# Accumulating DMAs from GpSimd in place of loads and sums, in a two-layer kernel with experts

## The reference

```python
xn = _layernorm(x)
s = _L0_attn_ref(xn, ...)
g = _silu(moe_experts(xn) + shared_mlp(xn))     # 8 of 64 experts per token, weighed, and the shared one
x = x + s * g
xn = _layernorm(x)
s = _L1_attn_ref(xn, ...)                       # causal attention over the batch axis of 2
g = _silu(_L1_ffn_ref(xn, ...))                 # two ternary linear layers with a gelu between
x = x + s * g
```

## Time and profile before

| | us |
|---|---|
| median of 3 timed runs | 412.49 (409.43 to 412.79) |
| the profiled execution | 405.89 |
| its span, first to last instruction | 404.1 |
| busy in the span: PE / DVE / ACT / POOL | 330.5 / 316.3 / 215.1 / 235.5 |

### The profile page before, as it was taken

One profiled execution on the slowest core, in us unless ns is written; L12 is line 12 of the kernel. 1 busy time (PEld: TensorE's weight loads), 2 busy tenths in 40 slices (PEclk: granted clock), 3 DMA queues, 4 the chain that ended last, 5 costly groups with the idle time before them and its releaser, 6 DMA issues.

```text
span 404.1 us, 6961 instructions
## 1 busy us (share of the span) xinstructions
PE 330.5 (82%) x2044; PEld 252.1 (62%) x2044; DVE 316.3 (78%) x989; ACT 215.1 (53%) x540; POOL 235.5 (58%) x219
## 2 busy tenths in 40 slices
PE   0999777989978989998898889970189888898893
PEld 0994344656666777776676667750068776787772
DVE  4589887766978888577878887742878998889975
ACT  3763535353544535854545454520286768766681
POOL 3610066666757877787887888762275765653311
PEclk9999999999999999999999999986589999999998
DMA  7965955667748899888877886557800000000001
GB/s 256 394 210 162 372 156 144 134 132 158 169 114 196 200 290 231 204 213 195 196 175 169 166 182 146 90 63 174 270 0 2 28 27 2 26 28 28 18 11 53
DMA packets 34041, 58.41 MB, mean 145 GB/s; under 512 B 3835, under 2 KB 20563, under 8 KB 33875
## 3 DMA queue, kind: packets, MB, share of 16 engines
q1 hardware_dynamic: 21715, 39.08, 30.1%
q0 software_dynamic: 12288, 18.88, 26.1%
HBM read 40.22 MB, written 17.73 MB: 143 GB/s over the span
## 4 chain that ended last, share of the span: by engine, by line
PE 32%; DVE 24%; issue 14%; POOL 11%; DMA 11%; ACT 7%; POOLq 0%; DVEq 0%; ACTq 0%
DMA acc_d<-W,idxE 8%; POOL acc_d L496 5%; PE two L1712 5%; POOL W L477 3%; PE two L1398 3%; PE two L1446 3%; PE two L1523 2%; PE two L1679 2%; PE two L1456 2%; PE two L1555 2%; PE two L1588 2%; DVE W L1106 2%; PE two L1474 2%; DVE WoS L977 2%; PE two L1408 2%
## 5 line engine op out<-in xcount | busy, mean ns | idle before, releaser
L496 POOL DMA_INDIRECT acc_d<-W,idxE x64 | 102.0, 1593 | 37.1 <-DVE W L1106 22.3
L477 POOL DMA_INDIRECT W<-tok_d,idxE x56 | 57.0, 1018 | 46.5 <-DVE idxE L1061 29.7
L707 ACT ACTIVATE W<-two 128x256 f32<-128x256 f32 x64 | 24.5, 384 | 72.9 <-PE two L1577 72.5
L1712 PE MATMUL two<-W,A 128*128 128x257 f16 x256 | 30.0, 273 | 10.7 <-DVE F L1328 9.9
L1712 PEld LDWEIGHTS two<-W,A 128*128 128x128 f16 x256 | 24.0, 98 | 16.3 <-DVE F L1328 11.7
L794 ACT ACTIVATE two<-two,gwv 128x512 f32<-128x512 f32 x32 | 21.3, 666 | 23.8 <-PE two L1679 23.8
L1679 PE MATMUL two<-F,wfcT 128*128 128x256 f16 x256 | 32.1, 280 | 1.4 <-DVE F L1266 1.4
L993 DVE TENSOR_TENSOR A<-two,A 128x512 f16<-128x512 f32 x32 | 22.0, 688 | 13.6 <-ACT A L684 13.3
L1149 DVE SCALAR_TENSOR_TENSOR W<-W,two 128x88 f32<-128x88 f32 x64 | 15.4, 241 | 20.9 <-ACT W L723 18.1
L1588 PE MATMUL two<-W 128*128 128x176 f32 x160 | 30.9, 316 | 0.2 <-ACT W L714 0.2
L1523 PE MATMUL two<-kT,vT 128*128 128x512 f32 x64 | 30.2, 594 | 0.0
(11 more groups left out here) (240 smaller groups left out, 898.7 us busy)
## 6 DMA issues: line engine op xcount, KB each, us to landing
W<-in_gu SPq DMA_DIRECT2D x20, 352.0 KB
acc_d<-F SPq DMA_DIRECT2D x2, 2176.0 KB, 14.6
F<-in_gu SPq DMA_DIRECT2D x12, 352.0 KB
W<-in_dn SPq DMA_DIRECT2D x20, 176.0 KB
tok_d<-xr SPq DMA_DIRECT2D x2, 1280.0 KB, 5.8
F<-in_dn SPq DMA_DIRECT2D x12, 176.0 KB
x<-in_q SPq DMA_DIRECT2D x4, 512.0 KB, 6.5
A<-in_Wo SPq DMA_DIRECT2D x1, 2048.0 KB, 13.0
```

Of the source, the lines that this page charges most:

```text
L477: pool.indirect_dma_start(out=xg[n % XR], out_offset=None, in_=tok_d[:, :], in_offset=bass.IndirectOffsetOnAxis(ap=idxE[:, n:n + 1], axis=0))\
L496: pool.indirect_dma_start(out=acc_d[n % 2][:, :], out_offset=bass.IndirectOffsetOnAxis(ap=idxE[:, n:n + 1], axis=0), in_=ysb[n % YS], in_o ...
L707: sc.activation(xgT[n % 2], bk_(2)[:, 0:D].rearrange("p (k n) -> p k n", k=KH), ACT.Copy)\
L1712: pe.matmul(z_bank(q_)[:, 0:D + 1], part[p % 2][:, at:at + P], wpj2[:, c, 0:D + 1], start=(c == 0 and part is hiT), stop=(c == FF1 // P - ...
```

## The change

For pairs 2 to 7 SP's loads of both accumulators and GpSimd's two sums go. In their place GpSimd issues two plain DMAs for each pair, which add the pair's rows of `acc_d[0]` and then of `acc_d[1]` onto the weighed shared rows in `xn`. The second of a pair waits until the first has landed. Three of the twelve are issued ahead of the loop; in the loop an iteration issues the second of one pair and the first of the next, after `add_gated` and before `finish`. `gated` and ACT's `gate` of a pair wait for both landings and read `xn` in place of `tot`. A semaphore `weighed` tells when DVE has weighed the shared rows.

```diff
@@ SP @@
             load_acc(1, 0)
             load_acc(1, 1)
-            for p in range(2, NP):
-                load_acc(0, p)
-                load_acc(1, p)
@@ GpSimd @@
-            def total(p):
+            def add_acc(i, p):
+
+                if p == 2:
+                    pool.wait_ge(acc_ld[1], 32)
+                    pool.wait_ge(weighed, NT // 4)
+                if i:
+                    pool.wait_ge(acc_ld[p], 16)
+                pool.dma_start(pair(xn, p), acc_v[i][:, 0:NT, :].rearrange("p (s i) d -> p s i d", s=2)[:, :, p, :],
+                               accum_op=ALU.add).then_inc(acc_ld[p], 16)
+
+            def gated(p):
+
+                pool.wait_ge(s0_ready, NT)
                 pool.wait_ge(acc_ld[p], 32)
-                then(pool.tensor_tensor(pair(tot, p), pair(tot, p), pair(acc1, p), ALU.add))
-
-            def add_shared(p):
-
-                pool.tensor_tensor(pair(tot, p), pair(tot, p), pair(xn, p), ALU.add).then_inc(acc_ready, 1)
-
-            def gated(p):
-
-                pool.wait_ge(s0_ready, NT)
-                pool.wait_ge(acc_ready, p - 1)
-                pool.tensor_tensor(pair(s0, p), pair(s0, p), pair(tot, p), ALU.mult).then_inc(gated_ready, 1)
+                pool.tensor_tensor(pair(s0, p), pair(s0, p), pair(xn, p), ALU.mult).then_inc(gated_ready, 1)
@@
+            add_acc(0, 2)
+            add_acc(0, 3)
+            add_acc(1, 2)
             for p in range(-AHEAD, NP):
                 if p >= 0:
                     weigh(p)
                 if 1 < p + AHEAD < NP:
-                    if p < 0:
-                        total(p + AHEAD)
-                        add_shared(p + AHEAD)
                     gated(p + AHEAD)
-                if 0 <= p and p + 1 + AHEAD < NP:
-                    total(p + 1 + AHEAD)
                 if p >= -2:
                     roots(p)
-                if p == -1:
-                    total(p + 1 + AHEAD)
-                if -1 <= p and p + 1 + AHEAD < NP:
-                    pool.wait_ge(own_ready, p + 2)
-                    add_shared(p + 1 + AHEAD)
                 if 0 < p + AHEAD < NP:
                     add_gated(p + AHEAD)
+                if -1 <= p and p + 1 + AHEAD < NP:
+                    add_acc(1, p + 1 + AHEAD)
+                if -1 <= p and p + 2 + AHEAD < NP:
+                    add_acc(0, p + 2 + AHEAD)
                 if 0 <= p < LAST:
                     finish(p)
@@ ACT, gate(p) @@
-                    sc.wait_ge(acc_ready, p - 1)
+                    sc.wait_ge(acc_ld[p], 32)
@@
-                    sc.activation(tg[p % 2][:, q_, :], tot[:, t, :], ACT.Tanh, scale=half_rden[:, t:t + 1]).then_inc(gate_ready, 1)
+                    sc.activation(tg[p % 2][:, q_, :], rows_[:, t, :], ACT.Tanh, scale=half_rden[:, t:t + 1]).then_inc(gate_ready, 1)
@@ DVE, shared_weighed @@
-                    last = mark(ve.tensor_scalar(xn[:, t, :], xn[:, t, :], den[:, t:t + 1], None, ALU.mult))
-                ve.wait_ge(dve, last)
+                    ins = ve.tensor_scalar(xn[:, t, :], xn[:, t, :], den[:, t:t + 1], None, ALU.mult)
+                ins.then_inc(weighed, 1)
@@ DVE, first_total @@
                 ve.wait_ge(acc_ld[p], 32)
+                ve.wait_ge(weighed, NT // 4)
```

More of the change, by code:

```diff
@@ L273, in build @@
         sc_ready, sig_ready = sem("sc_ready"), sem("sig_ready")
-        tot_first, silu_first, x1_first = sem("tot_first"), sem("silu_first"), sem("x1_first")
+        weighed, tot_first, silu_first, x1_first = sem("weighed"), sem("tot_first"), sem("silu_first"), sem("x1_first")
         xT_ps, xT_ready, logits_ps, tanh_ready, bks_ready = [sem(n) for n in (
@@ L290, in build @@
             "sc_ps", "nmax_ready", "probs_ready", "pT_ps", "pT_hi_ready", "pT_lo_ready", "o_ps", "oT_ready", "wo_ps", "s0_ready")]
-        acc_ready, gated_ready, gate_ready, silu_ready, x1_ready, xh_ready, xT1_ps, xT_hi_ready, xT_lo_ready = [
-            sem(n) for n in ("acc_ready", "gated_ready", "gate_ready", "silu_ready", "x1_ready", "xh_ready", "xT1_ps",
+        gated_ready, gate_ready, silu_ready, x1_ready, xh_ready, xT1_ps, xT_hi_ready, xT_lo_ready = [
+            sem(n) for n in ("gated_ready", "gate_ready", "silu_ready", "x1_ready", "xh_ready", "xT1_ps",
                              "xT_hi_ready", "xT_lo_ready")]
@@ L499, in _ @@
                     .then_inc(y_added[n % 2], 16)
-            def total(p):
-                pool.wait_ge(acc_ld[p], 32)
-                then(pool.tensor_tensor(pair(tot, p), pair(tot, p), pair(acc1, p), ALU.add))
-            def add_shared(p):
-                pool.tensor_tensor(pair(tot, p), pair(tot, p), pair(xn, p), ALU.add).then_inc(acc_ready, 1)
+            def add_acc(i, p):
[6 more added lines that the diff above has]
+                               accum_op=ALU.add).then_inc(acc_ld[p], 16)
             def gated(p):
                 pool.wait_ge(s0_ready, NT)
-                pool.wait_ge(acc_ready, p - 1)
-                pool.tensor_tensor(pair(s0, p), pair(s0, p), pair(tot, p), ALU.mult).then_inc(gated_ready, 1)
+                pool.wait_ge(acc_ld[p], 32)
+                pool.tensor_tensor(pair(s0, p), pair(s0, p), pair(xn, p), ALU.mult).then_inc(gated_ready, 1)
             def add_gated(p):
@@ L760, in gate @@
                 if p >= 2:
-                    sc.wait_ge(acc_ready, p - 1)
+                    sc.wait_ge(acc_ld[p], 32)
                 else:
                     sc.wait_ge(tot_first, p + 1)
+                rows_ = xn if p >= 2 else tot
                 if p == 2:
```

## The result

The changed kernel takes 415.46 us (414.67 to 415.97, 4 runs) against 410.96 us before (407.83 to 412.79, 4 runs): ratio 1.0151, 95% interval 1.0097 to 1.0205. It is slower, by less than forecast: 415.46 where 420.5 stood, inside the range of 411 to 426. The medians are 4.5 us apart; the ratio is taken from the runs in the chip's faster state, not from the medians, and is 6.2 us of 410.96. Its interval is clear of no change; whether the loss reaches the forecast's 2% these runs leave open.

The account below looks back on a forecast made before the run. Bound: a chain of waits through DVE, returning once per pair to GpSimd's pow. Terms 5.4 + 1.1 + 0.6 + 1.35 − 0.3 = +8.2 us on the 412.49 median gave 420.5 us; range 411 to 426.

Parts of the forecast that it names:

- the steady pair: Iterations of pairs 1, 2, 3: removed sums worth nothing, two issues delay the pow; 1.8 us longer each, +5.4 for three.
- three named effects: Steady pairs: PE's transposes wait for the weighing, DVE's L1309 for the square sums, and the product holds DVE's L1311.
- its signs: Expected in the profile: intervals of 14.8 us, first pow near 289, ramp's L1244 and L1200 at 0.17; wrong if weighing done before 320.
- rival 1: GpSimd's issue is as cheap as a gather, 0.99 us, slot 1.29, landing 4.4: +4.5, so 417.0; chance 0.30.
- the slot of an issue: GpSimd's time per adding DMA: 1.59 us as for a scatter-add, plus 0.30 gap, so 1.89.
- The forecast's own case: Issue of 1.2 to 2.2 us on GpSimd, whole kernel +5.5 to +14; chance 0.44.
- Pair 4: Iteration with one issue: the landing at 361.0 delays the product, and the pow starts at 362.3, not 361.24: +1.1.
- The first three issues: Ahead of the loop: the third waits for the first landing and holds pair 0's pow, its result late by +1.35.
- The 0.3 us from the unshared loads: Start of layer 1: pair 0's last load no longer shares queues with the dropped loads; 0.3 us gained, bounds 0 and 0.6.
- Pair 0 and the ramp: Iteration of pair 0: the ramp's 1.3 us head start is eaten, the pow starts at 309.8 instead of 309.24: +0.6.
- rival 3: Faster: slot at most 0.64 us, landing within 3, steady pairs lose nothing, ramp's 1.3 us stay: −1.9, 410.6; chance 0.19.
- The median: Base of the forecast: median of three timed runs, 412.49 us; the same sum on it gives 420.5.

Follow-up runs that it names:

- e7: Changed kernel with loop issues behind the pow and DVE's normalisation, third early issue behind the first pow: ratio to before 0.9969, layer 1 stretch 121.49 us.
- p1: Changed kernel with the twelve GpSimd DMAs as plain copies, without the addition: layer 1 stretch 121.74 us, intervals 12.96 to 12.98.
- e9: Changed kernel with the product behind DVE's normalisation and the weighing ahead of `finish`, issues unmoved: interval with two issues 12.95 us, layer 1 stretch 123.21.
- e2: Changed kernel with only the third of the first three issues moved behind the first pow: start 7.00 us, layer 1 stretch 126.88.
- e1: Changed kernel with the loop's DMA issues moved behind the pow, ahead of the residual sum: ratio to before 1.0081, layer 1 stretch 124.43 us.
- e3: Changed kernel with loop issues behind the pow and the third early issue behind the first pow: ratio to before 1.0075, layer 1 stretch 123.27 us.
- e8: Changed kernel with the product, from pair 0 on, behind the pow and DVE's normalisation: interval with two issues 13.51 us, layer 1 stretch 124.43.
- e4: Changed kernel with the product, from pair 0 on, behind the pow: first three intervals 15.09, 14.57, 15.20 us, layer 1 stretch 131.02.

## Why the forecast was right, and where its sizes were off

**Right: the sign and the mechanism.** The sums were hidden in the steady pairs, and e7 and p1 show what their going is worth there: 13.01 to 12.95. The added issues sat ahead of `finish`, weighing and product, and each of the three named effects is in the trace: PE waits for the weighing, DVE for the square sums, the product holds a short DVE instruction. Of its signs, the weighing ends behind 320 (5.56 us behind the residual sum, so 320.96 in the times of the earlier trace rows), and L1244 and L1200 of the ramp are short. e9 removes the two parts and gets all of the loop's loss back. Which short instruction the product holds changes: the forecast has L1311, and in the iterations of pairs 2 and 4 it was L1244 (L1242 now), which the forecast names only in rival 1.

**Mis-sized: the slot of an issue.** I took 1.89 us, the scatter-add with its gap of 0.30; it is 1.24 with no gap. That is the term of the sum that failed, and the rest of the steady pair follows from it: weighing 1.3 us earlier than forecast (5.56 instead of 6.9 behind the residual sum), pair +0.74 to +1.05 instead of +1.8, three of them +2.7 instead of +5.4. Rival 1, the price of a gather, had the slot (1.29) and the size per pair (1.1) about right; its +4.5 is nearer to the +5.3 than my +8.2. "Same operation" was the wrong nearness: the direct adding issue with twice the rows is cheaper than the indirect one. That the indices are the reason is likely but not shown; no run has an indirect issue without them. The range was wide enough to hold both cases. The forecast's own case began at an issue of 1.2 us and +5.5; measured are 1.24, +5.3 in the stretch, +4.5 between the medians and +6.2 by the ratio. So the total stands on its lower edge, and the time alone does not tell it from rival 1 (chance 0.30).

**Pair 4:** +1.1 forecast, +0.93 and +0.99 measured, and the nearness is partly luck. The landing decides, as forecast, but it came sooner: the product started 4.5 us behind its issue's start and 5.7 behind the residual sum (367.54 − 361.83), where 5.0 and 6.6 were forecast. It was to end last and let the `pow` follow at once; it ended 0.75 us ahead of the `pow`, having held L1242 for 1.12 us in place of 0.17.

**The first three issues:** +1.35 forecast, +1.26 measured, and e2 shows the place. Two sizes made up for one another here: the first issue began 0.98 us behind DVE's first total and not 0.45, and the third took 1.21 us and not 1.59. The 0.3 us from the unshared loads can't be read off: DVE's first total came 3.60 us behind SP's issue of the second loads before and 3.51 in the changed profile.

**Pair 0 and the ramp:** +0.6 forecast, +0.35 measured. The working has a slip: the landing at 303.4 + 5.0 is 308.4 and not 308.2, so the term should have read +0.8. The product did start where it was forecast, 6.25 us behind the residual sum (312.58 − 306.33; forecast 6.3), and it did hold L1310. The residual sum of pair 2 did come 1.2 us earlier against the end of the first `pow` (303.18 − 288.74 = 14.44 before, 306.33 − 293.10 = 13.23), where 1.3 was forecast. But with the loop's issues out of the way (e1, e3, e7, e8) the ramp falls only to 19.74 to 19.81: 0.7 of the 1.2 are left at the `pow`. The forecast and rival 3 counted 1.3. What holds the other 0.5 is not shown.

**The median:** the forecast stood on 412.49, and the median before came to 410.96 with the fourth run; 1.5 us of its miss are that (and 412.49 + 8.2 is 420.7, not 420.5). The stretch's +5.3 on 410.96 gives 416.3, against 415.46 measured.

**A rule that this trace tests.** In e1 a fp32 `tensor_scalar` of DVE from SBUF to SBUF took 0.60 us longer beside two GpSimd issues, which took their usual 2.47. The Trainium skill, "SBUF — State Buffer", section "SBUF: two separate sides", describes a lock between a DVE instruction in a two-port mode (its example is a float32 `tensor_copy` from SBUF to SBUF) and GpSimd's writing of descriptors, and warns of the DMA that is starved. Here GpSimd's issue kept its length and DVE lost, which may be the same lock from the other end; in which mode DVE ran no run shows. DVE was not held for the whole issue either: it was done at 330.82, the second issue at 331.16. The same section has DVE instructions with two SBUF inputs excluded by a GpSimd instruction that reads SBUF, for its whole length; 1.22 us instead of 0.16 at L1310, and e4's 1.24 instead of 0.17, agree. L1242 has one SBUF input and was held as long (1.27 and 1.12 instead of 0.17); by that section it would have to be in a two-port mode, which no run shows. The fit of the Trainium skill, "DMA: Bandwidth & Descriptors", section "Anatomy of one DMA — SWDGE (gpsimd) path" (2.6 us as an estimate for 256 KB), is under both measurements, 3.2 for the plain copy and 4.9 with the addition.

**Open.** e3 and e7 differ by 1.8 us in the stretch, but by 4.3 us in their timed ratios (1.0075 and 0.9969 of the kernel before) and by 5.4 in their medians (413.26 and 407.9). The other 2.5 to 3.6 us do not lie in the stretch. The moving start is a candidate: e3's profile has two stretches of 0.97 in the granted clock among the experts where e7's has 1.00, and its first total comes 4.5 us later. Why one kernel should fall into it more often than the other, when neither edit touches the experts, is not shown.

## What to carry to other kernels

Work that leaves an engine with time to spare is worth nothing there; work that is added to it is paid for according to what is queued behind it, so look for the engine's idle gap first, and for a part of it in which no neighbour is held by the issue (e7: the same DMAs, and layer 1 is 6 us shorter than changed). Where GpSimd and DVE share a stage, a late GpSimd instruction has two prices, its own lateness and the short DVE instructions it lands on; test them together and apart, for either can hide the other. Compare a stage by an anchor inside the execution when its start moves by more than the effect, and look at the granted clock of an interval before giving its length to the edit (e4).

## What the runs showed of the hardware

- A direct adding DMA of 256 rows of 1 KB takes GpSimd 1.24 us, a plain one 0.76, an adding one of 128 rows 0.90 (by the span of four). They land after 4.9, 3.2 and 3.8 us.
- No gap of 0.30 us stands between two direct issues, as it does between the indirect ones of the earlier trace rows.
- A GpSimd DMA issue holds up a DVE normalisation on SBUF: 1.33 us in place of 0.73 beside two issues. Beside the last half microsecond of a single one it was 0.79 in e1, and 0.73 in e7 beside a single one (290.08 to 291.29, the normalisation from 290.74). DMA engines 97% busy without an issue left it at 0.73. I had not expected that of an issue, and it cost e1 and e3 half a microsecond per pair.
- A GpSimd sum or product of 1.27 us that starts just ahead of a DVE instruction of 0.16 to 0.17 us on SBUF holds that to its own end: 1.22, 1.24 and 1.27 us. What it costs is what is left of the GpSimd instruction: 0.40 where DVE came late to it.
- The granted clock fell to 0.50 (1.2 GHz) in e4 behind 2 us in which PE was busy for 0.66, and 32 matmuls took 5.25 us in place of 3.71.
